# Four groups of on-chip transposes pulled together in a one-core gated cross-attention and mixture layer

## The reference

```python
x = x + tanh(g_xattn) * xattn(layernorm(x), ctx)
x = x + tanh(g_ffn) * ffn(layernorm(x))

def xattn(text, features):                 # one head over all 1024 features
    fn = rmsnorm(features, fn_w)
    Q = rmsnorm(text @ Wq.T + bq, qn_w)
    K = rmsnorm(fn @ Wk.T + bk, kn_w)
    return softmax(Q @ K.T / 32) @ fn

def ffn(x):
    base = x @ W_base.T + b_base           # 1024 x 1024
    gate = softmax(x @ W_gate.T)           # 8 experts
    w = relu(gate - sigmoid(x @ W_thr + b_thr) / 8), normalised over the experts
    h = x @ A_w.T                          # 8 experts of rank 16: 128 columns
    return base + 2 * ((h * w) @ B_w)      # the low-rank part
```

## Time and profile before

| | |
|---|---|
| median of 3 runs | 470.49 us |
| the profiled execution | 470.91 us |
| span of the profiled execution, first to last instruction | 469.1 us |
| PE busy | 464.3 us, 99% |
| DVE busy | 360.1 us, 77% |
| ACT busy | 172.6 us, 37% |
| POOL busy | 119.6 us, 26% |
| mean busy share of the 16 DMA engines | 49% |

### The profile page before, as it was taken

The page is one execution under the profiler, slowest core; times in us unless marked ns, Lnnn a source line. Parts: engine busy times, 40 slices in busy tenths (PEclk is TensorE's granted clock), DMA queues, the critical chain, the costliest instruction groups (busy, mean ns, idle before and its releaser), DMA issues.

```text
span 469.1 us, 6945 instructions
## 1 busy us (share of the span) xinstructions
PE 464.3 (99%) x2481; PEld 398.3 (85%) x2481; DVE 360.1 (77%) x750; ACT 172.6 (37%) x349; POOL 119.6 (26%) x107
## 2 busy tenths in 40 slices
PE   8999999999999999999999999999999999999997
PEld 7898999998888888888888887888888888888886
DVE  1777996868889968779988887967758678875833
ACT  4947541341224214226335426332241521413400
POOL 0021511003344353336253306031040502205000
PEclk9999999999999999999999999999999999999999
DMA  8995129857577378577379640220504131050202
GB/s 308 410 411 228 80 91 376 341 180 294 191 254 248 134 247 293 198 283 240 149 265 421 286 143 37 73 109 13 169 0 136 45 109 71 2 179 1 90 1 90
DMA packets 22114, 84.40 MB, mean 180 GB/s; under 512 B 2624, under 2 KB 3904, under 8 KB 19264
## 3 DMA queue, kind: packets, MB, share of 16 engines
q1 hardware_dynamic: 21792, 83.81, 49.1%
q10 hardware_dynamic: 288, 0.15, 0.1%
HBM read 61.93 MB, written 22.02 MB: 179 GB/s over the span
## 4 chain that ended last, share of the span: by engine, by line
PE 91%; DMA 6%; DVE 2%; issue 0%; ACT 0%; DVEq 0%; SPq 0%
PE bank L664 11%; PE bank L784 9%; PE bank L788 9%; PE bank L786 9%; PE bank L700 7%; PE bank L702 7%; PE bank L701 7%; PE bank L757 4%; PE bank L545 4%; DMA bt_raw<-bt_dram 3%; DMA out_dram<-xs 2%; PE bank L686 2%; PE bank L685 2%; PE bank L687 2%; PE bank L736 2%; PE bank L737 2%
## 5 line engine op out<-in xcount | busy, mean ns | idle before, releaser
L1575 POOL TENSOR_TENSOR small<-small,tiny 128x1 f32<-128x1 f32 (+2 forms) x25 | 23.6, 942 | 167.7 <-DVE small L1201 140.6
L1555 DVE SCALAR_TENSOR_TENSOR xs<-bank,tiny,xs 128x512 f32<-128x512 f32 (+1 forms) x61 | 43.1, 739 | 24.1 <-PE bank L788 18.5
L700 PE MATMUL bank<-xth,gram 128*128 128x512 f32 x144 | 57.3, 398 | 0.0
L702 PE MATMUL bank<-xtl,gram 128*128 128x512 f32 x144 | 56.2, 390 | 0.0
L701 PE MATMUL bank<-xth,gram 128*128 128x512 f32 x144 | 56.1, 390 | 0.0
L1603 POOL TENSOR_TENSOR sq_sum<-sq_sum,sq 128x512 f32<-128x512 f32 x24 | 32.0, 1332 | 57.1 <-DVE sq L1383 57.1
L784 PE MATMUL bank<-wh_T,zh 128*128 128x512 f32 (+1 forms) x116 | 46.1, 397 | 0.4 <-DVE xs L1555 0.4
L784 PE MATMUL bank<-wh_B,zh 128*128 128x512 f32 x116 | 46.3, 399 | 0.0
L788 PE MATMUL bank<-wh_B,zl 128*128 128x512 f32 x116 | 45.3, 391 | 0.0
L786 PE MATMUL bank<-wl_B,zh 128*128 128x512 f32 x116 | 45.2, 390 | 0.0
L788 PE MATMUL bank<-wh_T,zl 128*128 128x512 f32 (+1 forms) x116 | 44.6, 384 | 0.0
(11 more groups left out here) (200 smaller groups left out, 1129.1 us busy)
## 6 DMA issues: line engine op xcount, KB each, us to landing
xst<-x_dram SPq DMA_DIRECT2D x16, 512.0 KB, 4.2
xz<-xt_dram SPq DMA_DIRECT2D x16, 512.0 KB, 7.9
out_dram<-xs SPq DMA_DIRECT2D x14, 512.0 KB, 2.7
xa<-x_dram SPq DMA_DIRECT2D x12, 512.0 KB, 4.2
x<-xa SPq DMA_DIRECT2D x12, 512.0 KB, 3.1
xs<-x SPq DMA_DIRECT2D x12, 512.0 KB, 4.0
wq_raw<-wq_dram SPq DMA_DIRECT2D x8, 512.0 KB, 14.0
t_raw_T<-wb_dram SPq DMA_DIRECT2D x4, 1024.0 KB, 16.1
```

The lines of the kernel that those rows point to most:

```text
L700: pe.matmul(acc[:, :], gram[:, g, 0, :], xth[b % 2][:, r, :], start=r == ROWS[j][0], stop=False)
L702: done = pe.matmul(acc[:, :], gram[:, g, 0, :], xtl[b % 2][:, r, :], start=False, stop=r == ROWS[j][-1])
L1555: dve.scalar_tensor_tensor(out=xs[slot][:, cols], in0=bank[n_bank][:, 0:hi - lo], scalar=tg[:, 1:2], in1=xs[slot][:, cols], op0=ALU.mult, ...
```

## The change

It moves stages in the list and adds or removes no instruction. In the last attention batch `zt(0, a12)` goes from ahead of y(3, 6) to ahead of y(3, 5), next to `zt(0, a11)`, and `zt(0, a22)` goes from behind y(3, 7) to ahead of it, next to `zt(0, a21)`. `joint` is now true for pair 1 too, and `zt(1, a12)` follows `zt(1, a11)` behind product 6 of pair 0. `mt 0` goes from behind product 1 of pair 0 to behind product 2, just ahead of `pt 3`. In the list, `stat` of tile 2 (the second tile of pair 1) stands behind product 1, after the place that `mt 0` had.

```diff
-        joint = [PLAIN < q < (NT - TPB) // 2 - 1 or q == NP - 1 for q in range(NP)]
+        joint = [PLAIN <= q < (NT - TPB) // 2 - 1 or q == NP - 1 for q in range(NP)]
...
                               3: [("bb",), ("bias", 0)],
-                              5: [("zt", 0, "a11"), ("stat", 1)],
-                              6: [("zt", 0, "a12"), ("xn", 1), ("head_w",)],
-                              7: [("zt", 0, "a21")]}.get(j, [])
+                              5: [("zt", 0, "a11"), ("zt", 0, "a12"), ("stat", 1)],
+                              6: [("xn", 1), ("head_w",)],
+                              7: [("zt", 0, "a21"), ("zt", 0, "a22")]}.get(j, [])
...
-        first += [("zt", 0, "a22"), ("load_xs", 1, 1), ("load_xs", 1, 0),
-                  ]
+        first += [("load_xs", 1, 1), ("load_xs", 1, 0)]
...
                              3: [("zt", q, "a21"), ("zt", q, "a22"), ("xn", t1), ("sum_high", q, "s1")],
-                             6: [("zt", q, "a11"), ("sum_high", q, "s3"), ("sum_high", q, "s2"), ("sum_low", q, "s1"),
-                                 ("sum_low", q, "s3"), ("bias", t1)],
-                             7: [("zt", q, "a12"), ("sum_low", q, "s2"), ("sum_high", q, "s4")]}
+                             6: [("zt", q, "a11"), ("zt", q, "a12"), ("sum_high", q, "s3"), ("sum_high", q, "s2"),
+                                 ("sum_low", q, "s1"), ("sum_low", q, "s3"), ("bias", t1)],
+                             7: [("sum_low", q, "s2"), ("sum_high", q, "s4")]}
...
-                         1: [("mt", 0)],
-                         2: [("pt", 3), ("load_bt",), ("fn_split", 3)], 3: [("w_load", "T3")], 4: [("fn_low", 3)],
+                         2: [("mt", 0), ("pt", 3), ("load_bt",), ("fn_split", 3)], 3: [("w_load", "T3")], 4: [("fn_low", 3)],
```

## The result

| | before | after |
|---|---|---|
| median of 5 runs each, us | 470.49 (470.21 to 471.04) | 472.63 (472.02 to 473.36) |
| the profiled execution, us | 470.91 | 473.36 |
| its span, us | 469.1 | 471.6 |

A forecast was written before the change was run, and what follows sets the result against it. PE, busy 464.3 of 469.1 us, was taken as the bound. 0.38 + 1.69 - 0.02 - 0.60 = +1.45, taken as +1.4 on the profiled 470.91, less its 0.42 above the median, gave 471.9 us, range 470.9 to 472.7.

The forecast's parts named there:

- What bounds: PE is full, busy 464.3 of 469.1 us; only less PE work or removing a rare wait can gain.
- A place of transposes: Merging two groups of four transposes on PE saves 0.01 to 0.09 us, taken as 0.02; four places are merged.
- Attention part: Low part of a12 ahead of stat 1 on DVE delays attend 10's banks; PE +0.38 us through pair 0's start.
- The 0.16 at attend 11: PE's present delay at attend 11's second pair goes because PE reaches it later: 0.16 us back.
- mt 0: DVE's `mtl` of tile 0 falls behind the statistics of tile 2; PE waits at zt(1, a21), +1.69 us.
- a12 of pair 1: Placing a12's transposes behind a11's in pair 1 saves 0.02 us; its bank is free over 1 us before.
- The wait that goes: PE's 0.60 us wait at 285.81 us for DVE's addition to xs goes, as PE comes later: -0.60 us.
- POOL in front: Rival, chance 0.12: a POOL addition slips ahead of fn_raw, the 0.60 wait stays or grows: +2.0, 472.5 us.
- No wait at attend 10: Rival, chance 0.15: DVE comes through its queue sooner, the 0.57 is not there: +0.9, 471.4 us.
- no wait for `mtl`: Rival, chance 0.08: the wait at zt(1, a21) does not grow, +0.38 stays: 470.9 us.
- faster: Rival, chance 0.05: each of four merges saves 0.09, waits at 236.43 and 285.81 go: -1.1, 469.4 us.
- The signs to look for: New PE waits on `mtl` (about 1.7 us) and `xa`, no xs wait, statistics ahead of `mtl`, 0.79 for eight transposes.

The follow-up runs named there:

- both_orders_kept: The changed kernel with statistics of tile 2 behind mt 0 and DVE's low part of a12 behind the emptying of attend 9: 471.06 us, ratio 1.0010.
- attn_only: The kernel before with only the attention part of the change: 471.20 us, ratio 1.0009.
- attn_low_later: The kernel before with only the attention part, and DVE's low part of a12 behind the emptying of attend 9: 470.79 us, ratio 1.0008.
- mt_only: The kernel before with only mt 0 moved next to pt 3: 472.58 us, ratio 1.0037.
- stat_first: The kernel before with mt 0 left in place and only the statistics of tile 2 put ahead of it: 472.29 us, ratio 1.0041.
- again: The changed kernel run once more with no edit: 472.90 us, ratio 1.0048.
- control: The kernel before run once more with no edit: 470.35 us, ratio 0.9995.
- a12_only: The kernel before with only a12 of pair 1 put next to a11: 470.68 us, ratio 1.0006.
- best: both_orders_kept, plus the statistics of pair 2's second tile put behind DVE's addition to xs: 470.49 us, ratio 0.9997 against the kernel before.
- mt_order_kept: The changed kernel with the statistics of tile 2 and the bias addition put behind mt 0: 470.93 us, ratio 1.0009.

## Why the prediction was right where it was, and off where it was

**What bounds.** Right. PE is full, and the two losses of the kernel after are waits of PE for DVE where the prediction put them.

**A place of transposes: 0.02 saved.** Inside its bounds of 0.01 to 0.09. A merged group takes 0.79 (220.04 to 220.83). From ahead of the group at 220.04 to 227.5 us, over the merge of a11 and a12, the lateness of after goes from 0.99 to 0.94. This is 0.05, since in before the matmuls behind a place keep a slightly longer step than the pace for some 2 us. The merge of mt 0 with pt 3 gives 0.02 in `both_orders_kept`. (The text of the prediction gives the two attention merges 0.04 and its sum takes 0.03; nothing hangs on it.) What the merges ahead of 253 us save can't reach the end: in before PE already waits there for `mtl`, and in the table's column "behind zt(1, a21)" nothing of it is left.

**Attention part: +0.38.** Right: 0.36 in both traces of after, 0.38 in `attn_only`. zt(0, a21) had been put 0.57 later, and is: 232.23 less 230.68 less 0.98. Shown by `both_orders_kept` and `attn_low_later`, which take it away. The 0.16 at attend 11 came back too (0.17). Overlooked was that a22's low part passes the last `sq`; here PE's own lateness covers that.

**mt 0: +1.69.** Right. zt(1, a21) was to be 2.07 late in all; it was 1.97 and 2.15. Alone the part costs 1.61, and DVE's order without any move on PE 1.90. The term itself is 1.69 in all four; the rest is when ACT's split of the weight block comes: -0.06 late in `mt_only`, 0.21 in `stat_first`, 0.29 in after and 0.45 in `again`. The prediction had taken PE's 0.38 for it, which is near, but it is ACT's and its load's lateness that counts here, and it differs between executions.

**a12 of pair 1: -0.02.** Right only with the rest: from 257 to 282 us the lateness of after falls by 0.06. Alone it costs about 0.1 by 282 us, for want of the cover that the late PE gave. (The 0.19 at the end of that trace is mostly the wait at 396 us.)

**The wait that goes: -0.60.** Right for the trace that it was read from, probably too large as a term of the sum. The wait does go (2.90 late at 287.32, 2.30 at 288.11). Its chain had been put 0.8 late; the addition ends 0.3 to 0.8 late in the four kernels with the long wait, start taken off. But the kernel before has it to very different sizes: 0.60 in the first trace and none in the control; among kernels that come to it less than 0.4 us late by the table's count, `a12_only` has 0.51, `both_orders_kept` 0.53 and `attn_only` about 0.2. It depends on how long loads take to land. From issue to landing the low-rank weights took 12.27 in before and 11.72 in the control, where the statistics that stand ahead of the addition started 0.09 sooner while PE was 0.68 later; in `a12_only` the weights took 11.88, but the `xs` load took 3.90 where it had been 3.21. The two columns at the right of the table tell the average: the end of the trace less the timed runs is -0.5 in the control and -0.1 to -0.8 in the other 12, with a mean of -0.4. All are against the same first trace of before, so by this estimate that execution was some 0.4 us above the average behind 215 us; it also lay 0.42 above the median of its runs (470.91 for 470.49). The prediction carried its sum over to that median and subtracted the whole 0.60, which the median may hold only in part. If the 0.4 is all of this wait, the average has 0.2, and the sum is +1.85, or 472.3. The five traces that come to it less than 0.4 late (0.60, 0.53, 0.51, 0.2 and 0) have 0.37 in the mean, which gives +1.7. The timed runs don't settle it: the edit that takes the wait away gives -0.2 on the kernel before, and -0.6 between `both_orders_kept` and `best`, which were timed on different chips.

**What stays open.** From +1.7 or +1.85 to the measured +2.1 and +2.3 is inside the intervals. The wait at 396 us (0 to 0.6, in seven of the 14 traces, early and late ones) may be part of it, and so may the landing of the load ahead of ACT's split; no run took either away.

**The rivals.** *POOL in front* would have left the wait at 286 us and made `fn_raw` long: `fn_raw` took 1.28 and the wait is gone. Its 472.5 is nearer to the measured 472.63 than the forecast of 471.9 all the same, by luck. The forecast itself is 0.7 low: its mechanism held, and the range took the rest in. *No wait at attend 10*, *no wait for `mtl`* and *faster* are ruled out by the rows at 231.01 and 256.72. The signs to look for were there: the two new waits, the turned order on DVE, 0.79 for a group of eight, no line on `xs` at 286 us. One of them was named in the wrong place: the attend wait shows in the distances alone and not in the list of waits.

## What to carry to other kernels

In a kernel whose engines all run through one list of stages, moving a stage moves it in every queue: look on each for what it passes, above all where a semaphore of the full engine hangs on a short instruction, since a long one slipped in front of that costs its whole length. Count a wait that a delay is to swallow by its size in several executions; where it hangs on the landing of a DMA, one trace gives one draw. A merge of short transposes gave 0.02 to 0.05 us of PE's time here, since nearly all of their price was in their number, and even that was lost at the next bank that PE waited for.

## What the runs showed of the hardware

A bank that comes late costs PE more than its lateness: after a wait the next matmul follows by 0.33 instead of 0.23 (231.01 to 231.34, and 230.34 to 230.68 in `attn_only`). Transposes started by such a wait take 0.85 to the next matmul (256.72 to 257.57) where the group without one takes 0.79.

Executions with the same instructions up to 215 us differ by up to 1.3 us in PE's starts there (-0.22 in `mt_order_kept`, 0 in the first trace of before, 1.11 in `a12_only`), at a granted clock of 0.999 to 1.0 over the whole span. A wait further on can take this back: the control was 0.76 late at 215 us and 0.05 at the end.

One load of one weight block, `wr_B`, took 5.4 us from issue to landing in the control, 6.15 in before and 6.26 in `attn_low_later`.
